# Four-layer graph network on one core: per-batch row tables, unspilled last groups, factors collected early, products one batch later

## The reference

```
h = relu(layernorm(x)); x = x + L0(h)     # cosine-weighted neighbour sum
h = relu(layernorm(x)); x = x + L1(h)     # 8 relations: softmax attention over edges, plus a self loop per node
h = relu(layernorm(x)); x = x + L2(h)     # edge MLP with a gate, segment sum and segment max, node MLP
h = relu(layernorm(x)); x = x + L3(h)     # GATv2 with 4 heads, batch norms, feed-forward
```

## Time and profile before

| | |
|---|---|
| median of three runs | 5163.74 us (5163.03 to 5171.63) |
| the profiled execution | 5164.5 us, its span 5162.7 us |
| busy share of the span | PE 52%, PEld 26%, DVE 76%, ACT 15%, POOL 69% |
| layer 1's last gather to layer 2's first | 2269.83 to 2403.35 us |
| last sums of layer 2 to layer 3's first gather | 3417.9 to 3541.5 us |
| DMA | 1040.87 MB, mean 202 GB/s |

### The profile page before, as it was taken

The page is one execution under the profiler, slowest core; times in us unless marked ns, Lnnn a source line. Parts: engine busy times, 40 slices in busy tenths (PEclk is TensorE's granted clock), DMA queues, the critical chain, the costliest instruction groups (busy, mean ns, idle before and its releaser), DMA issues.

```text
span 5162.7 us, 62058 instructions
## 1 busy us (share of the span) xinstructions
PE 2708.5 (52%) x10695; PEld 1349.2 (26%) x10695; DVE 3942.5 (76%) x10565; ACT 790.2 (15%) x2017; POOL 3537.6 (69%) x3645
## 2 busy tenths in 40 slices
PE   5844267436775000014444444455777887728992
PEld 3532122114664000012111111122333333313331
DVE  8866999546999986645777777755878788889993
ACT  0000022110000025521222222220000000003331
POOL 4777777744777877766777777755777777715652
PEclk7555577667999555557777667768999888969996
DMA  9420167313222146634888888836999999938990
GB/s 348 146 90 9 59 222 256 128 64 118 53 54 53 41 143 201 201 94 168 287 284 280 295 282 282 289 122 239 308 313 309 313 308 310 310 107 302 332 321 21
DMA packets 458297, 1040.87 MB, mean 202 GB/s; under 512 B 129581, under 2 KB 247829, under 8 KB 427884
## 3 DMA queue, kind: packets, MB, share of 16 engines
q1 hardware_dynamic: 167018, 580.42, 31.2%
q0 software_dynamic: 131968, 217.09, 14.9%
q10 hardware_dynamic: 159234, 242.47, 13.6%
HBM read 560.07 MB, written 477.20 MB: 201 GB/s over the span
## 4 chain that ended last, share of the span: by engine, by line
POOL 39%; issue 19%; PE 18%; DVE 13%; DMA 10%; DVEq 1%; ACT 1%; POOLq 0%; ACTq 0%; SPq 0%
POOL arena L692 22%; POOL weights L731 16%; DMA arena<-tab,ring 8%; PE psum L1296 6%; PE psum L1297 5%; PE psum L1372 3%; DVE arena L2222 1%; DVE arena L1681 1%; DVE arena L1946 1%; PE psum L1126 1%; DVE arena L2051 1%; DVE arena L2037 1%; DVE arena L2055 1%; DVE arena L1831 1%; PE psum L1347 1%
## 5 line engine op out<-in xcount | busy, mean ns | idle before, releaser
L692 POOL DMA_INDIRECT arena<-tab,ring x2352 | 2307.4, 981 | 717.3 <-issue 697.2
L1296 PE MATMUL psum<-arena,ident 128*128 128x512 f32 x1176 | 729.2, 706 | 821.9 <-DMA arena<-tab,ring 628.8
L1681 DVE SCALAR_TENSOR_TENSOR arena<-arena,ns 128x64 f32<-128x64 f32 (+2 forms) x2351 | 869.3, 370 | 203.2 <-ACT arena L925 58.0
L731 POOL DMA_INDIRECT weights<-arena x784 | 806.2, 1028 | 291.1 <-issue 238.7
L1297 PE MATMUL psum<-arena,ident 128*128 128x512 f32 x1176 | 680.3, 663 | 0.0
L1296 PEld LDWEIGHTS psum<-arena,ident 128*128 128x128 f32 x1176 | 248.6, 224 | 1201.8 <-issue 1014.5
L800 POOL TENSOR_TENSOR arena<-arena,score 128x256 f32<-128x256 f32 x294 | 230.5, 809 | 257.4 <-issue 123.4
L1372 PE MATMUL psum<-arena,ident 128*128 128x512 f32 x784 | 361.9, 607 | 63.7 <-DVE arena L2222 63.1
L2151 DVE SCALAR_TENSOR_TENSOR arena<-psum,rowb 128x1024 f32<-128x1024 f32 x196 | 239.1, 1220 | 196.7 <-PE psum L1297 196.2
L1297 PEld LDWEIGHTS psum<-arena,ident 128*128 128x128 f32 x1176 | 256.9, 218 | 348.1 <-issue 348.1
L1260 PE MATMUL psum<-agg,arena 128*128 128x200 bf16 x2352 | 237.8, 251 | 117.7 <-DVE arena L1804 117.7
(11 more groups left out here) (416 smaller groups left out, 4142.2 us busy)
## 6 DMA issues: line engine op xcount, KB each, us to landing
put<-zero SPq DMA_DIRECT2D x98, 1040.0 KB
arena<-put SPq DMA_DIRECT2D x98, 1040.0 KB
spill<-arena ACTq DMA_DIRECT2D x98, 1024.0 KB, 5.3
arena<-spill SPq DMA_DIRECT2D x98, 1024.0 KB
state<-arena ACTq DMA_DIRECT2D x147, 512.0 KB
weights<-zero SPq DMA_DIRECT2D x32, 1600.0 KB, 18.4
arena<-weights SPq DMA_DIRECT2D x32, 1600.0 KB, 7.7
put<-zero SPq DMA_DIRECT2D x14, 3584.0 KB
```

What stands on the lines that cost most here:

```text
L692: pool.indirect_dma_start(out=rows[:, h, k, :], out_offset=None, in_=table[:, :], in_offset=bass.IndirectOffsetOnAxis(ap=ring[:, h, word + ...
L731: pool.indirect_dma_start(out=weights0[:, :], out_offset=bass.IndirectOffsetOnAxis(ap=words0[:, g, k:k + 1], axis=0), in_=words0f[:, g, K ...
L1296: pe.matmul(place, lhsT=ident[:, :], rhs=rows_of[0][:, s, columns, 0:width], start=True, stop=False)
L1681: beats.add(dve.scalar_tensor_tensor(out=rows[:, s, k, :], in0=before, scalar=mark(ns, g, k), in1=rows[:, s, k, :], op0=ALU.mult, op1=ALU. ...
```

## The change

Four edits. (1) Layer 1's last four groups are neither spilled nor loaded: `messages1` reads them from `g1` where the gathers left them, so `kept` counts one less per slot in everything that follows. (2) `rows2` and `rows3` are written in five pieces, each behind its batch's table. (3) GpSimd collects the factors of batches 0 and 1 after the last gather and before `whole_segments`, those of batches 2 to 4 after it. (4) In `mix(2, ...)` the narrow products move from the first part to the second, and VectorE's narrow sum with them; in the passage to layer 3, `mix3(b)` and its copies move one batch later on all three engines, and its five narrow products stand before tile 4.

```diff
 def after(n, s):
-    return {1: 0, "2": 1, "3a": 2, 3: 3}[n] * groups_at(s)
+    return {1: 0, "2": 1, "3a": 2, 3: 3}[n] * groups_at(s) - (0 if n == 1 else 1)
+def last1(g):
+    return isinstance(g, int) and g >= NG - 4
...
 # SyncE
-                if late(g, 3):
+                if late(g, 3) and not last1(g - 3):
                     spill1a(g - 3, (s - 3) % 4, before_of(g, s, uses, 3)[0])
-            quads(sp, load1a)
-            for g in range(NG - 3, NG):
-                spill1a(g, g % 4, g // 4)
+            quads(sp, load1a, apart=4)
...
+                at = bass.ds(b * NB, NB)
+                sp.dma_start(rows2.rearrange(by_node, i=NT)[:, at, :], bn_rows[:, at, :]).then_inc(rows_out, 16)
             for b in range(NBATCH):
                 table2(b)
-            sp.dma_start(rows2.rearrange(by_node, i=NT), bn_rows).then_inc(rows_out, 16)
...
+                at = bass.ds(b * NB, NB)
+                sp.dma_start(rows3.rearrange(by_node, i=NT)[:, at, :], xr_rows[:, at, :]).then_inc(rows_out, 16)
             for b in range(NBATCH):
                 table3(b)
-            sp.dma_start(rows3.rearrange(by_node, i=NT), xr_rows).then_inc(rows_out, 16)
...
 # GpSimd
+            ready((beta_out, 16), (weights_set, 1))
+            collect_batches(betas, eidx, beta_n, loops_in, range(0, 2))
             whole_segments(1, state1, 1, open_sum[:, 0:D])
-            ready((beta_out, 16))
-            collect_batches(betas, eidx, beta_n, loops_in)
+            collect_batches(betas, eidx, beta_n, loops_in, range(2, NBATCH))
             collect_batches(state1, eidx, agg, arrived)
...
 # ScalarE
-                act.wait_ge(loaded[s], use * 16 + 16)
+                rows = g1 if last1(g) else gc1
+                if last1(g):
+                    act.wait_ge(got[s], 16 * K * groups_at(s))
+                else:
+                    act.wait_ge(loaded[s], use * 16 + 16)
...
-                load1c(g, s, uses)
+                if not last1(g):
+                    load1c(g, s, uses)
...
                 deviation_of(7 + b, b)
+                if b:
+                    rows3_of(b - 1)
                 if b < NBATCH - 1:
                     hidden2(b + 1)
                 need(act, mixed_a, 10 + NB * b)
                 lift_turned(place(5, b), hT_c)
-                rows3_of(b)
+            rows3_of(NBATCH - 1)
...
 # TensorE
-                    if narrow is not None and lo == 0:
+                    if narrow is not None and (lo == 0) == (s == 1):
...
             def out2(b):
-                need(pe, taken_a, 10 + 3 * (b - 1) + 1 if b else 0)
+                need(pe, taken_a, 10 + 3 * (b - 1) if b > 1 else 0)
...
             def mix3(b):
-                turn_from(place(5, b), hst_c)
                 pe.wait_ge(lifted, place(5, b) + 1)
                 for j in range(NB):
-                    pe.matmul(bank(3)[:, NB * D + j * 2 * H:NB * D + (j + 1) * 2 * H], lhsT=hT_c[:, j, :],
-                              rhs=wla_full[:, :, :].rearrange("d a h -> d (a h)"), start=True, stop=True)
-                for j in range(NB):
+                    if j == 4:
+                        pe.wait_ge(taken, 20 + min(b + 2, NBATCH))
+                        for i in range(NB):
+                            pe.matmul(bank(3)[:, NB * D + i * 2 * H:NB * D + (i + 1) * 2 * H], lhsT=hT_c[:, i, :],
+                                      rhs=wla_full[:, :, :].rearrange("d a h -> d (a h)"), start=True, stop=True)
...
                     turn2(b + 1)
+                if b:
+                    mix3(b - 1)
+                if b < NBATCH - 1:
                     mlp2(b + 1)
-                mix3(b)
+                turn_from(place(5, b), hst_c)
+            mix3(NBATCH - 1)
...
 # VectorE
-                    if lo == 0:
+                    if lo:
+                        dve.wait_ge(taken_a, 5 + b + 1)
                         beats1n.done(dve.tensor_tensor(xn[:, at, :], xn[:, at, :], product(5 * 512, NB * D, D), ALU.add))
...
-                    if j == 0:
+                    if j == 4:
                         linear = bank(3)[:, NB * D:NB * D + NB * 2 * H].rearrange("p (j a) -> p j a", a=2 * H)
...
+                if b:
+                    nodes3(b - 1)
                 if b + 2 < NBATCH:
                     stage2(b + 2)
-                nodes3(b)
+            nodes3(NBATCH - 1)
```

22 lines of the change are left out of this document (11 added, 11 removed).

## The result

The changed kernel takes 5140.22 us (median of six runs, 5131.31 to 5143.49) against 5163.59 for the kernel before (six runs beside it, 5159.1 to 5171.63): a ratio of 0.9952 [0.9943, 0.9962], faster by 23.4 us. Its profiled execution took 5139.28 us, with a span of 5137.5 against 5162.7.

A forecast was written before the change was run, and what follows sets the result against it. GpSimd's row gathers were taken as costliest and untouched; between passes, chains of waits through all engines bound the kernel. 14 + 7.4 + 4.9 = 26 us off 5163.7 gave 5138 us, range 5126 to 5152.

The forecast's parts named there:

- Unspilled groups: Layer 1 to 2 passage: the last group's write and load go, 4.7 us, so the last sums leave at 2278.1.
- Ten factor reads: Layer 1 to 2 passage: ten reads delay GpSimd's open read to 2284.4, so 1.3 of the 4.7 us remain there.
- Narrow products: Layer 1 to 2 passage: VectorE's first part begins at 2294.9, 7.7 us earlier; a batch takes 8.9 us instead of 10.46.
- I take 6.2 in all, no more, since batch 1 will wait some 2 us for TensorE: Layer 1 to 2 passage: shorter batches give 6.2 us; with 7.7 us earlier start, 14 us, bounds 9 and 17.
- TensorE warm throughout: Rival for both passages: TensorE's clock stays at 1.0, 4 us more gained, 5134 us; chance 0.16.
- rows2 in pieces: Layer 1 to 2 passage: writing the rows in pieces was taken as nothing, bounds -1 and +1 us.
- Products one batch later: Layer 2 to 3 passage: gain only at the first batch, steady batches stay near 13.1 us; 7.4 us, bounds 0 to 9.
- 1.0 more for a clock not yet full: Layer 2 to 3 passage: 1.0 us added to three batch-to-batch stretches of 13.1 us each, reaching 3500.4.
- the batch of delay is lost: Rival, layer 2 to 3 passage: clock near 0.8, 14.7 us a batch, the 7.4 us gone, 5146 to 5150; chance 0.16.
- The slower rival: Both passages: TensorE stays at 1.2 GHz, waiting inside the products for VectorE's copy; +22 us, 5186; chance 0.03.
- rows3 in pieces: Layer 2 to 3 passage: read after the scatters follows the last rows by 9.0 us instead of 13.9; 4.9 us, bounds 2 and 5.5.
- That an edge pass gives the time back I rule out: Edge passes: lengths stay, as gathers are queued behind one another; a change over 2 us would mean a missed coupling.

The follow-up runs named there:

- the second profile: The changed kernel profiled again, unaltered; its five runs beside that took 5143.65 us, ratio 0.9958 to the kernel before.
- the version with both steps: Changed kernel with eight early factor reads instead of ten, and the next batch's hidden layer ahead of tiles 3 and 4; 5132.62 us, 0.9935 to the kernel before.

## Why the prediction was right, point by point

The forecast of 5138 us, its side and its case were right; 5140.2 is inside the range. The sum of 26 us stands against 28.1 in the two passages and 25.2 in the spans. That it came out so close is in part luck: the first passage gave 4.6 us more than forecast and the reordered products 2.6 less, and 2.9 us of the rest went to stretches that the sum had left out. In the second profile the passages gave 31.9 us, and 6.6 went there.

- *Unspilled groups*: sums at 2278.1, or 8.3 us behind the last gather; measured 7.9. Right.
- *Ten factor reads*: the open read was to come 14.6 us behind the last gather, 1.3 earlier than before; it came 13.7 behind, 2.2 earlier. I had charged 0.7 us for the waits and 0.9 for a last read, and the profile has the plain pace of 1.25 us and 0.30 of idle time. That the reads overshoot the sums by some 3 us was right, and eight reads got 2.5 of them.
- *Narrow products*: the first product of VectorE at 25.1 us behind the last gather (2294.9); measured 24.5. The batch 8.9 us; measured 8.4 to 8.7.
- *"I take 6.2 in all, no more, since batch 1 will wait some 2 us for TensorE"*: this is the step that failed in the first passage. Batch 1 did not wait: TensorE's clock rose during its narrow products at 2290.96 (1.50 us for the ten, 2.40 in the earlier trace rows), and the first parts after that took 2.84 us where the sum had reckoned with slower ones. From VectorE's first product to its fifth it took 34.4 us instead of 44.0, so the batches gave 9.5 us, not 6.2. With 8.8 up to the first product, 0.7 lost in the last batch, which now holds the narrow sum, and 1.0 behind the node products the first passage gave 18.6 us instead of 14, above even the bound of 17. The cause of the 1.0 stays open; it is 1.2 in the second profile and 0.2 in the version with both steps. For this passage the rival "TensorE warm throughout" came true (0.97 against 0.79).
- *rows2 in pieces*: nothing, and the read waits 2.2 us as before, with pieces and, in the run that undid them, without.
- *Products one batch later*: "in the steady part the change wins nothing" was right, 12.8 to 13.1 us for a ring at full clock against 13.0 to 13.1, and so was the place of the gain: the second sum 9.7 us behind the first, measured 9.8 in the first profile at a clock of 0.58, and 6.7 in the second at 1.00. The last rows came 4.8 us earlier in the first profile and 8.4 in the second, around the 7.4 forecast. What failed is the term for the clock, "1.0 more for a clock not yet full": the clock was full in two rings and fell in the fourth, which took 16.2 us in both profiles instead of 13.1, and the end took 19.3 instead of 18.1. Here a piece of the rival "the batch of delay is lost" came true.
- The slower rival, TensorE at 1.2 GHz through both passages, did not come: VectorE's copy makes TensorE wait 1.70 us in each ring after the first, and the clock stayed at 1.00 over two rings of that kind. The rule of the Trainium skill (TensorE: Matmul & The Clock Gate, A second HAM failure mode) fits the fall in the fourth ring, but it says as much of the two before it, which stayed at full clock.
- *rows3 in pieces*: 4.9 us forecast, 4.7 measured, twice, and gone again when the part was undone. By the rule in the Trainium skill (DMA: Bandwidth & Descriptors, Bandwidth) the gain would have been nearer to 2. The pieces do cost more in sum, as it says: each landed 4.3 us after its issue, five times that is 21.5 us, and the one write took 11.5. But only the last piece lies on the path, and the other four lie beside computation, so the trace decides against the smaller gain.
- *"That an edge pass gives the time back I rule out"*, with 2 us as the bound: layer 3's gathers, from the first to the last, took 3.5 and 3.2 us longer in the two profiles (1008.7 and 1008.4 against 1005.2), so by its letter the statement fell. No coupling was found; the gathers' own spread from one version to another, 977 to 984 ns in the mean, is larger than my bound.

## What to carry to other kernels

Work that fits into an engine's wait is free only up to the moment that the wait would end: count the instructions against it (ten reads came to the open read 5.8 us behind the last sums, eight 3.4, and the sums want 3.0). When two engines take turns on the same banks, move whatever the waiting one does not need first behind its first part; that turned 10.46 us a batch into 8.6. Before delaying a stage by one batch, write out which steps leave the ring and which enter it: here they were equal in length and the gain was one batch's worth, until the order inside the ring was changed so that TensorE's wait for a copy was filled, which brought the ring from 12.8 to 11.1 us. A large write behind the last computed row is worth cutting even into pieces that move at a lower rate (4.3 us for 650 KB, 11.5 for 3250), since only the last one is waited for.

## What the runs showed of the hardware

- Where GpSimd's open read is the first indirect DMA behind its gather loop, the write after it comes 5.7 to 5.9 us behind it; with eight or ten other reads between the loop and them it comes 3.5 to 3.7 us behind. The write then follows VectorE's sum by 0.9 us instead of 3.1. How long the engine idled before (15 or 967 us in the one case, 0.3 or 336 in the other) makes no difference.
- TensorE's clock came up earlier in one execution of the same kernel than in another (0.58 and 1.00 over the same ring), and the second passage was 3.7 us shorter with it. It fell in the fourth ring, at the same place, in both (0.50 from 3472.6 to 3479.3, at full clock until then), and not in the one profile of a version that left TensorE no such wait. In the first passage waits of 1.3 to 1.4 and 0.6 to 0.8 us a batch stood beside a clock of 1.00 for 40 us, and waits of 2.6 us, in the kernel before, beside a clock that fell once in each batch.
- On some chips or at some times the same kernels took 7.7 ms instead of 5.15, with unchanged instructions and long idle stretches that end with "issue" or "remote". The variants' ratios to the kernel before were still 0.994 to 0.998 there.
